# Halves or whole groups: the streams of the first layer of a two-layer decoder

## The reference

```python
x = x + L0_attn(layernorm(x))      # A
x = x + L0_xattn(layernorm(x), ctx, ctx)   # B
x = x + L0_ffn(x)                  # C, D, experts

# A: q = tanh(x Wc + bc), one number a token; shell = l2norm(x Ws + bs), 64 numbers
#    proj = shell omega + bias;  phi_s = [cos(proj), sin(proj)]
#    phi  = (mags * q**[0..4]) outer phi_s, times W_combine -> 64 numbers
#    logits = phi phi^T * decay / temp, causal; softmax; times V; times W_out
# B: one head: q Wq, k = ctx Wk, v = ctx Wv, softmax over 361, times v
# C: h = layernorm(y) with scale and shift; causal attention of 16 heads of 16; wo
# D: h = layernorm(...); scores = h gate_w (8 experts); the two best and a softmax over them
#    experts: silu(h w1) * (h w2), then w3, of 512 hidden, weighted by the gate
```

## Time and profile before

| | us |
|---|---|
| median of the runs | 1693.62 |
| lowest to highest of 3 runs | 1688.9 to 1701.72 |
| profiled execution | 1689.45 |
| its span | 1687.8 |
| front of group 0 alone | 71.2 |
| three woven stretches | 122.9, 123.6, 125.6 |
| rear of group 3 alone | 77.1 |

### The profile page before, as it was taken

One profiled execution on the slowest core, in us unless ns is written; L12 is line 12 of the kernel. 1 busy time (PEld: TensorE's weight loads), 2 busy tenths in 40 slices (PEclk: granted clock), 3 DMA queues, 4 the chain that ended last, 5 costly groups with the idle time before them and its releaser, 6 DMA issues.

```text
span 1687.8 us, 24678 instructions
## 1 busy us (share of the span) xinstructions
PE 1285.4 (76%) x7936; PEld 890.2 (53%) x7936; DVE 998.3 (59%) x2156; ACT 522.3 (31%) x1279; POOL 415.1 (25%) x528
## 2 busy tenths in 40 slices
PE   2677868767877699981458977779787697986987
PEld 1554654644644366651237754467554475644755
DVE  4447557457455233325676765768656686677852
ACT  2214324324322222210125512346213363233620
POOL 1032143243253200006622111311212212032100
PEclk9778878878888799995679989779897799987988
DMA  9510010191014211101315310044100350104501
GB/s 376 217 28 1 19 28 13 34 408 49 25 46 198 59 47 44 44 29 45 117 39 98 86 40 12 10 101 111 40 12 2 86 122 21 32 11 88 114 5 46
DMA packets 69693, 122.37 MB, mean 73 GB/s; under 512 B 25404, under 2 KB 55100, under 8 KB 68032
## 3 DMA queue, kind: packets, MB, share of 16 engines
q1 hardware_dynamic: 63936, 110.04, 21.7%
q0 software_dynamic: 5632, 10.77, 2.3%
HBM read 67.69 MB, written 53.07 MB: 72 GB/s over the span
## 4 chain that ended last, share of the span: by engine, by line
PE 46%; issue 24%; DVE 12%; POOL 8%; DVEq 3%; ACT 3%; DMA 2%; POOLq 2%; SPq 0%; ACTq 0%
PE ps L1143 7%; PE ps L1390 5%; PE ps L1162 3%; PE ps L525 3%; PE ps L1316 3%; PE ps L1332 3%; PE ps L533 2%; POOL experts L1779 2%; PE ps L1302 2%; PE ps L1403 2%; PE ps L933 1%; PE ps L1041 1%; POOL headbd L681 1%; PE ps L504 1%; DVE probs L1999 1%
## 5 line engine op out<-in xcount | busy, mean ns | idle before, releaser
L1628 ACT ACTIVATE probs<-ps,small 100x361 f32<-100x361 f32 x256 | 141.3, 557 | 94.1 <-DVE small L2347 89.5
L2347 DVE TENSOR_REDUCE small<-ps 100x2 f32<-100x722 f32 x128 | 115.7, 906 | 36.2 <-PE ps L1302 36.2
L1143 PE MATMUL ps<-every,xT_t 128*128 x256 | 122.3, 601 | 0.4 <-issue 0.4
L1390 PE MATMUL ps<-hT,experts 128*128 128x400 f32 x288 | 117.1, 558 | 1.2 <-DVE small L730 1.2
L1316 PE MATMUL ps<-cst,probs 100*121 100x100 f32 x768 | 104.0, 271 | 8.1 <-DVE probsT L2355 7.7
L1316 PEld LDWEIGHTS ps<-cst,probs 100*121 100x121 f32 x768 | 94.8, 185 | 22.2 <-issue 13.7
L2355 DVE TENSOR_SCALAR probsT<-ps 121x600 f32<-121x600 f32 x128 | 99.2, 775 | 9.1 <-PE ps L1316 9.1
L1332 PE MATMUL ps<-probsT,values_ 121*32 121x100 f32 x1536 | 90.8, 253 | 0.9 <-DVE probsT L2355 0.9
L1302 PE MATMUL ps<-k_stack,q_stack 96*100 96x362 f32 x256 | 81.8, 400 | 6.3 <-ACT probs L1628 5.6
L473 POOL TENSOR_TENSOR small<-small,cst 100x2 f32<-100x2 f32 x56 | 11.1, 198 | 295.3 <-DVE small L453 295.2
L1390 PEld LDWEIGHTS ps<-hT,experts 128*128 128x128 f32 x288 | 59.6, 215 | 42.2 <-issue 14.1
(11 more groups left out here) (329 smaller groups left out, 2887.2 us busy)
## 6 DMA issues: line engine op xcount, KB each, us to landing
k_stack<-key_d SPq DMA_DIRECT2D x192, 90.5 KB, 3.1
tok_d<-wt SPq DMA_DIRECT2D x1, 14848.0 KB, 45.5
res_d<-wt SPq DMA_DIRECT2D x1, 14848.0 KB, 42.0
every<-e_d SPq DMA_DIRECT2D x8, 1536.0 KB, 11.6
ctxT<-ctxT_d SPq DMA_DIRECT2D x8, 726.0 KB, 4.3
key_d<-k_hi SPq DMA_DIRECT2D x32, 181.0 KB, 2.8
key_d<-k_lo SPq DMA_DIRECT2D x32, 181.0 KB, 3.4
gates<-gate_d SPq DMA_DIRECT2D x28, 200.0 KB, 4.4
```

The lines of the kernel that those rows point to most:

```text
L1143: ins = e.matmul(ps[:, 2 * i + t % 2, :], xT_t[:, t % 2, c, :], every[:, bass.ds(base + (i * DC + c) * HID0, HID0)], start=(c == 0), stop= ...
L1390: ins = e.matmul(bank(2 * i + j % 2, n=NT), w[:, c, :], hT[:, c, :], start=(c == 0), stop=(c == DC - 1))
L1628: ins = e.activation(f_e[:, n % 2, i, 0:LC], bank(2 * (n % 2) + i, S, LC), ACT.Exp, bias=h_nm[:, n % 2, i:i + 1], accum_out=h_sum[:, b, h: ...
L2347: inc(e.tensor_reduce(h_nm[:, n % 2, 0:2], ps[0:S, 2 * (n % 2):2 * (n % 2) + 2, 0:LC], AX, ALU.max, negate=True), "F_nm")
```

## The change

Both parts of the first layer become one stream for a whole group each. `early(g)` has the steps of `early(g, h)`, each for four sequences: one DVE instruction over 400 or 4 x n columns where there were two, one ACT evacuation of a whole group, one POOL power of 100 x 4 for two of 100 x 2. Instructions that stand once for each sequence (statistics, `xn`, exponentials, matrix products of 100 rows) stay as many. `behind(g)` likewise has one step where it had one for each half, and 28 steps instead of 36. `woven(front, rear)` issues, in each of 18 rounds, one front step and then as many rear steps as `REAR_STEPS` says: two in rounds 0 to 3, one in 4 to 6, two in 7 to 12, one in 13 to 17. The attention's 19 steps now lie at rear steps 4 to 22, rounds 2 to 12.

PSUM: the front has banks 0 to 3 as one set, the rear 4 to 7. `A_in` and `A_comb` of all four sequences lie in banks 0 to 3 at once. Names of the first layer are declared with `wholes` and signalled once for a group. The transposed probabilities of B leave in two ACT copies of two sequences each instead of four. `recips_pool` of half 0 moves on POOL from behind the attention into its step 12. SP's three waits are for the whole group's signals; its loads are the same. The front of group 0 is issued as one stream with nothing beside it (`list(early(0))`).

The helpers are `norm4_dve`, `root4_pool`, `turn4_pe`, `turn4_act`, `projT4_pe`, `proj4_pe`. The core of the diff follows: the driver, the helpers, PE's first front steps and its rear up to the attention, two details on ACT and POOL, DVE's `phi`, and DVE's rear.

```diff
-ROUNDS, STEPS = 18, 19
+REAR_STEPS = (2, 2, 2, 2, 1, 1, 1, 2, 2, 2, 2, 2, 2, 1, 1, 1, 1, 1)
+STEPS = 19
...
-def woven(x0, x1, y):
-
-    for _ in range(ROUNDS):
-        for st in (x0, y, x1, y):
-            next(st)
+def woven(front, rear):
+
+    for steps in REAR_STEPS:
+        next(front)
+        for _ in range(steps):
+            next(rear)
...
+        def wholes(name, phase1, phase3="", sem_name=None):
+
+            sem = ctx.enter_context(nc.semaphore(sem_name or name))
+            for i, p in enumerate(phase1):
+                names[f"{p}_{name}"] = Signal(sem, len(phase1), i)
+            for i, p in enumerate(phase3):
+                names[f"{p}_{name}"] = Signal(sem, 2 * len(phase3), len(phase1) * NG + 2 * i, 2)
...
+        def norm4_dve(e, pre, g, src, xn_out):
+
+            stats, mv, _, r1, _, _ = for_y if pre in ("C_", "D_") else for_x
+            for b in range(NB):
+                e.bn_stats(stats[:, b, :], src[:, b, :])
+            e.drain()
+            for b in range(NB):
+                ins = e.bn_aggr(mv[:, b, :], stats[:, b, :])
+            inc(ins, pre + "mv")
+            e.drain()
+            yield
+            W(e, pre + "rstd", g)
+            for b in range(NB):
+                ins = e.tensor_scalar(xn_out[:, b, :], src[:, b, :], mv[:, b, 0:1], r1[:, b:b + 1],
+                                      ALU.subtract, ALU.mult)
+            return ins
+
+        def root4_pool(e, pre, g, eps2=None):
+
+            _, mv, var_e, r1, r2, t1 = for_y if pre in ("C_", "D_") else for_x
+            W(e, pre + "mv", g)
+            e.tensor_tensor(var_e, mv[:, :, 1], cs("eps", S)[:, 0:NB], ALU.add)
+            e.drain()
+            ins = e.tensor_tensor(r1, var_e, cs("mhalf", S)[:, 0:NB], ALU.pow)
+            if eps2 is not None:
+                e.drain()
+                e.tensor_tensor(t1, r1, r1, ALU.mult)
+                e.drain()
+                e.tensor_tensor(t1, t1, mv[:, :, 1], ALU.mult)
+                e.drain()
+                e.tensor_scalar(t1, t1, eps2, None, ALU.add)
+                e.drain()
+                ins = e.tensor_tensor(r2, t1, cs("mhalf", S)[:, 0:NB], ALU.pow)
+            inc(ins, pre + "rstd")
+
+        def part4(b0):
+
+            return ps[:, b0:b0 + 2, 0:NT]
...
+        def turn4_pe(e, pre, g, name, b0, src, ready, half=0):
+
+            W(e, ready, g, 1, half)
+            for c in range(DC):
+                for b in range(NB):
+                    ins = e.transpose(ps[:, b0 + c, b * S:(b + 1) * S], src[:, b, c * P:(c + 1) * P], identS)
+            inc(ins, pre + name)
...
+        def projT4_pe(e, w, src, b0, name):
+
+            for m in range(DC):
+                for c in range(DC):
+                    ins = e.matmul(bank(b0 + m, n=NT), w[:, c, m * P:(m + 1) * P], src[:, c, :],
+                                   start=(c == 0), stop=(c == DC - 1))
+            inc(ins, name)
+
+        def proj4_pe(e, w, srcT, b0, name):
+
+            for b in range(NB):
+                for c in range(DC):
+                    ins = e.matmul(ps[0:S, b0 + b // 2, b % 2 * D:(b % 2 + 1) * D], srcT[:, c, b * S:(b + 1) * S],
+                                   w[:, c, :], start=(c == 0), stop=(c == DC - 1))
+            inc(ins, name)
...
 
-            def early(g, h):
-                p, q, t, bs = 2 * h, 2 * h + 1, tok(h), list(enumerate(seqs(h)))
-                yield
-                turn_pe(e, "A_", g, h, "hTp", p, xnX, ("A_xn", 1))
-                yield
-                W(e, "A_hT", g, 1, h)
+            def early(g):
+                yield
+                turn4_pe(e, "A_", g, "hTp", 0, xnX, "A_xn")
+                yield
+                W(e, "A_hT", g)
                 w = wv("A_in", DC)
-                for i, b in bs:
+                for b in range(NB):
                     for c in range(DC):
-                        ins = e.matmul(bank(p + i, S, 321), hTX[:, c, b * S:(b + 1) * S], w[:, c, :],
+                        ins = e.matmul(bank(b, S, 321), hTX[:, c, b * S:(b + 1) * S], w[:, c, :],
                                        start=(c == 0), stop=(c == DC - 1))
                 inc(ins, "A_in_p")
...
+                    ins = e.matmul(bank(b, S, 320), a_trig[:, b * S:(b + 1) * S], wv("A_comb", rows_=SH),
                                    start=True, stop=True)
                 inc(ins, "A_comb")
...
                         scores(n)
@@ -1081,42 +1137,38 @@
                 yield
                 if routed:
                     ahead(g - 1)
-                yield
-                for h in range(2):
-                    turn_pe(e, "C_", g, h, "hTp", 4 + 2 * h, xn, ("C_xn", 1))
-                    yield
-                for h in range(2):
-                    W(e, "C_hT", g, 1, h)
-                    if h == 1 and routed:
-                        e.wait_ge(r_placed.sem, r_placed.at(g - 1))
-                    proj_pe(e, h, wv("C_v", DC), hT, 5 + 2 * h, "C_vp")
-                    projT_pe(e, h, wv("C_k", DC), hT, 4 + 2 * h, "C_kTp")
-                    yield
-                for h in range(2):
-                    W(e, "C_v", g, 1, h)
-                    projT_pe(e, h, wv("C_q", DC), hT, 5 + 2 * h, "C_qTp")
+                turn4_pe(e, "C_", g, "hTp", 4, xn, "C_xn")
+                yield
+                W(e, "C_hT", g)
+                if routed:
+                    e.wait_ge(r_placed.sem, r_placed.at(g - 1))
+                proj4_pe(e, wv("C_v", DC), hT, 6, "C_vp")
+                projT4_pe(e, wv("C_k", DC), hT, 4, "C_kTp")
+                yield
+                W(e, "C_v", g)
+                projT4_pe(e, wv("C_q", DC), hT, 6, "C_qTp")
                 yield
                 yield from attend(g)
-                for h in range(2):
-                    turn_pe(e, "C_", g, h, "rTp", 4 + 2 * h, xn, ("C_rx", 1))
-                    yield
-                for h in range(2):
...
-                W(e, "B_pTp", g, 1, h)
-                for i, b in enumerate(seqs(h)):
-                    ins = e.activation(b_eT[:, b, :], bank(p + i, KW, KC * S), ACT.Copy)
+                W(e, "B_pTp", g)
+                for b in range(0, NB, 2):
+                    ins = e.activation(b_eT[:, b:b + 2, :], ps[0:KW, b:b + 2, 0:KC * S], ACT.Copy)
...
+                    if n == 12:
+                        recips_pool(e, "C_", g, 0, 1)
...
-                W(e, "A_comb", g, 1, h)
-                W(e, "A_q", g, 1, h)
-                phi = a_phi[:, o, :]
-                qb = a_q[:, o].unsqueeze(2).broadcast_to([S, HB, SH])
-                pm = lambda m: ps[0:S, p:p + 2, m * SH:(m + 1) * SH]
-                e.tensor_scalar(phi, pm(ORD - 1), MAGS[ORD - 1] / MAGS[ORD - 2], None, ALU.mult)
+                W(e, "A_comb", g)
+                W(e, "A_q", g)
+                qb = a_q.unsqueeze(2).broadcast_to([S, NB, SH])
+                pm = lambda m: ps[0:S, 0:NB, m * SH:(m + 1) * SH]
+                e.tensor_scalar(a_phi, pm(ORD - 1), MAGS[ORD - 1] / MAGS[ORD - 2], None, ALU.mult)
                 e.drain()
                 for m in range(ORD - 2, -1, -1):
                     if m == ORD - 2:
-                        e.tensor_tensor(phi, phi, qb, ALU.mult)
+                        e.tensor_tensor(a_phi, a_phi, qb, ALU.mult)
                     else:
-                        e.scalar_tensor_tensor(phi, phi, MAGS[m + 1] / MAGS[m], qb, ALU.mult, ALU.mult)
+                        e.scalar_tensor_tensor(a_phi, a_phi, MAGS[m + 1] / MAGS[m], qb, ALU.mult, ALU.mult)
                     e.drain()
-                    ins = e.tensor_tensor(phi, phi, pm(m), ALU.add)
+                    ins = e.tensor_tensor(a_phi, a_phi, pm(m), ALU.add)
                     if m:
                         e.drain()
                 inc(ins, "A_phi")
                 yield
...
                 ways = route(g - 1) if routed else iter(())
                 group = xall[:, bass.ds(g * NB, NB), :]
-                norms = [norm_dve(e, "C_", g, h, group, y) for h in range(2)]
-                next(norms[0])
+                norm = norm4_dve(e, "C_", g, group, y)
+                next(norm)
                 next(ways, None)
                 yield
-                next(norms[1])
-                yield
-                for h in range(2):
-                    list(norms[h])
-                    e.drain()
-                    for b in seqs(h):
-                        ins = e.tensor_scalar(xn[:, b, :], y[:, b, :], r2Y[:, b:b + 1], None, ALU.mult)
-                    inc(ins, "C_xn")
-                    if h == 0:
-                        next(ways, None)
-                    yield
-                for h in range(2):
-                    W(e, "C_vp", g, 1, h)
-                    inc(e.tensor_scalar(c_v[:, own(h), :], tokens(5 + 2 * h), 1.0, None, ALU.mult), "C_v")
-                    yield
+                list(norm)
+                e.drain()
+                for b in range(NB):
```

(40 more changed lines are left out.)

423 lines of the change are left out of this document (197 added, 226 removed).

## The result

The changed kernel took 1736.69 us (median of 4 runs, 1736.21 to 1741.99), the kernel before 1691.69 us in the runs beside it. The ratio is 1.0262 with a 95% interval of 1.0214 to 1.0310: 45 us slower. The profiled execution has a span of 1735.1 us against 1687.8, so 47.3 us more.

The account below looks back on a forecast made before the run. PE was taken as nearest to a bound, 93 of 124 us busy in a woven stretch. Woven +12.3, front +20, rear +3.6 made +35.9 us: 1689.45 to 1725.4 profiled, 1729 as median, range 1686 to 1754.

Parts of the forecast that it names:

- the wait for `A_shn`: Rounds 2 to 6 of a woven stretch: PE waits over 3 us for this input from DVE; a 4 us gap.
- the front alone: Front of group 0 with nothing woven in, 71.2 us before: engines' times add to 91, +20 us.
- the woven stretches: Three stretches weaving one group's rear with the next front: +4.1 us each, 12.3 together, 126 to 130 long.
- the waits for Sin and `phi`: Rounds 4 and 5 of a woven stretch: PE waits 2 and 2.4 us by the sum, over 3 each as sign.
- (a): Woven stretch, first statistics to first attention scores, 32.4 us before: -0.7 us.
- (b): Woven stretch, first attention scores to stage A's logits in round 7, 25.1 us before: +3.9 us.
- (c): Woven stretch, stage A's logits to last attention values, rounds 7 to 12, 39.8 us before: +2.2 us.
- (d): Woven stretch, last attention values to the next group's statistics, 26.3 us before: -1.3 us.
- rear alone: Rear of group 3 with nothing woven in, 77.1 us before: end is a bare chain, +3.6 us.
- B: Rival for the whole kernel: DVE's chain is the bound everywhere, so not slower; 1677 us, chance 0.17.
- C: Rival: weaving is even, gaps in (b) and (c) paid by (a) and (d), only ends lose; 1706 us, chance 0.20.
- D: Rival: PE's clock falls and stays, +10 us a woven stretch, ends +28; 1752 us, chance 0.15.

Follow-up runs that it names:

- steps_late: Changed kernel, rear steps reordered: one in rounds 0 to 2, two in 3 to 12, one in 13 to 17; 1717.01 us, ratio 1.0140 to the kernel before.
- steps_early: Changed kernel, rear steps reordered: two in rounds 0 to 9, one in 10 to 17; 1751.08 us, ratio 1.0358 to the kernel before.
- tail_warm: Changed kernel with filler matrix products on PE in the last rear only; 1738.21 us, ratio 1.0271 to the kernel before.
- rear_halves: Changed kernel with the rear back in half streams, 36 steps, two a round, front whole; 1710.71 us, ratio 1.0086 to the kernel before.
- warm_all: Changed kernel with filler matrix products on PE in group 0's front alone and in the woven rounds; 1733.64 us, ratio 1.0232 to the kernel before.

## Why the prediction held, point by point

The direction, the size and the range were right: 1729 predicted, 1736.7 measured, slower by more than 1%. Part of that is luck. The sum is a worse forecast than its total: it put the first layer at +36 where +60 were measured, and the total came near because code that it took as unchanged was 12.6 us shorter. Of the signs named ahead, the wait for `A_shn`, round 10 and DVE's busy time came; the front alone (85 to 95 us), the woven stretches (126 to 130) and the waits for Sin and `phi` (over 3 us) did not. What the sum had too small is in each of these places mostly one term, PE's work at the lower clock. By its own terms, against profiled stretches:

| term | predicted | measured |
|---|---|---|
| front alone | +20 (8 to 24) | +25.9 |
| (a) of a woven stretch | -0.7 | -0.8 |
| (b) | +3.9 | +4.8 |
| (c) | +2.2 | +6.9 |
| (d) | -1.3 | -0.9 |
| three woven stretches | +12.3 | +25.8 |
| rear alone | +3.6 | +7.9 |
| first layer | +35.9 | +60 |
| code behind it | 0 | -12.6 |

- **Front alone.** The mechanism was right: in one stream the engines' times add. The sum of 93 less 2 of overlap came to 97.1. PE's work grew to 53.0 at a clock of 0.68, 5.1 more than the 47.9 of the earlier trace rows that the sum had kept. ACT was busy 15.8 and not 12.4: the sum took off three table loads, but both kernels have three in this stretch. More overlap than 2 us hid a part of that. The upper bound of 95 for half clock throughout does not follow from its own lower bound: if full clock takes 12 us off PE's 47.9, half clock makes them about 72, and the bound about 115.
- **(a), (b) and (d)** were each within 1 us. In (a) the terms add up to 32.4, no change; the -0.7 was set lower for the stretch in which nothing is routed, so that the routed one gave -0.8 is chance. In (b) the wait for `A_shn` is there with 4.6 us, as forecast; those for Sin and `phi` are 2.1 and 2.0, near the 2 and 2.4 of the sum and not over 3. PE's front steps of rounds 3 to 6 began 6.4, 12.8, 17.7 and 26.1 us after the first scores, where 6.4, 13.0, 17.8 and 24.5 were predicted; the last is late behind a round at a clock of 0.60. The reason given for (b), one rear step as too little cover, is not borne out as it stands: (a) and (b) of `steps_late`, with two rear steps in rounds 4 to 6, are together 4.0 us shorter, but `steps_early`, also with two, is 12.0 longer in (b).
- **(c) is the step that failed.** Its rounds 7, 9 and 10 were counted well (7.2, 6.2 and 11.7 us; 7.9, 6.5 and 12.0 predicted), but with 0.4 us for the clock in the whole part. Round 10, from `A_out` to the next transposes:

```profile
331.98 3.71 PE L535 MATMUL ps<-wt,experts 128*100 128x256 f32 x16
...
343.70 1.60 PE L509 MATMUL ps<-cst,experts 100*128 100x100 f32 x8 [1.28 <-DVE experts L478]
```

  PE was busy 37.8 us there at 0.78, against 31.7 at 0.96 in the earlier trace rows: 6.1 of the 6.9 us. Round 8 took 6.9 us for 5.0 predicted, at 0.55, and rounds 11 and 12 took 14.7 for 10.2, at 0.59; the same instructions in the same order took 5.5 and 11.6 in `steps_late`. The clock term of (c) was thus about 4.4 and not 0.4. The sum took (c)'s clock over from before, though it placed new gaps on PE in the same rounds and had seen in the earlier trace rows that a gap can bring the lower level.
- **Rear alone.** The tail of whole steps grew by 7.3 us (23.2 from the last values to the routing, 15.9 before), where 3.1 was predicted; the 21.6 in the expectation of `tail_warm` is too small. `C_out` was costed at 3.5, full clock, and took 6.6; the gate's scores, costed at 1.6 in (d), took 2.8. These two make up the 4.2 us that the sum lacked. `tail_warm` did not test whether full clock would give them back, as its filler stood in the way.
- **POOL.** `root4_pool`'s power of 100x4 took 1.05 us, between the bounds of 0.75 and 1.5 and near the 1.2 taken:

```profile
L488 POOL TENSOR_TENSOR small<-small,cst 100x4 f32<-100x4 f32 x4 | 4.2, 1050 | 1.6 <-issue 1.5
```

- **DVE** saved 30.3 us of busy time in the first layer, 24 predicted, while every stretch grew.
- **The code behind** was taken as unchanged. It was 12.6 us shorter, and that hid half of the error in the first layer. Nothing in the prediction leads there.
- **The rivals.** B, DVE's chain as the bound, is excluded: DVE's busy time fell and every stretch grew. C, woven stretches even, is what `steps_late` (376.1) and `rear_halves` (377.0) come to, not the changed kernel. D, the clock falls and stays, put the stretches at +10 each, the first layer at +58 and the total at 1752. In the profile the woven stretches rose by 8.6 each with the clock at 0.77, and the first layer by 60: by place and size D is closer to the first layer than the forecast, and only the shorter code behind it put the total on the forecast's side. D's cause is shown for (c), by 4.4 of its 6.9 us. It is not shown for all: with the clock back at 0.83 in `warm_all` two thirds of the loss stayed, about half of that from its filler by the estimate above, and `steps_late` has 0.78 in a stretch only 2.8 us longer than before. The rule of the Trainium skill cited with D ("TensorE: Matmul & The Clock Gate", section "HAM oscillation — how this bites in real kernels"), that idle gaps send the array back to half rate, agrees with these rows as far as the lower clock goes.

## What to carry to other kernels

Two interleaved half streams are each other's cover: made into one, every engine's step stands in the open wherever nothing else is woven in, and that price (26 and 8 us at the two ends here) did not depend on the order of the woven steps, while the saved fixed cost per instruction (30 us on DVE) shortened no stretch, as DVE was not the bound. In a hand-written order the list of steps is as large a lever as the steps: the same instructions took 376 to 434 us, so a change of grain has to be timed with its order tried anew, not with the first list that fits. Cost every matmul behind a gap at both clocks. Filler is a test of the clock only where it fits its gap: it was worth 9 us in one stretch, and in another it delayed the chain by as much as it gave. Two kernels that issue the same instructions in the same order from some point on are the cleaner test.

## What was not expected of the hardware

- Code with the same instructions took 1111.5 to 1125.2 us over the kernels of this study, with granted clocks of 0.87 and 0.95 on the same 40 us of attention, and with stalls of 6 us on DVE that no semaphore explains. Runs of one kernel scatter as much (1687.2 to 1705.2 us for the kernel before), while the three woven stretches of the changed kernel's code took 397.8 or 397.9 us in three builds. A difference under 14 us between two profiled executions is not evidence about the edit until the stretch that was edited is cut out.
- Mean clock and length part ways: from 0.77 to 0.83 by filler gave 3.3 us of 133.6 in a woven stretch, and from 0.80 to 0.84 none in the last rear, while another order of the steps gave 7.2 us at 0.78.
- An order of steps reaches beyond itself: rounds 8, 11 and 12, the same in every instruction, took 4.4 us less in `steps_late`, at clocks of 0.69 and 0.79 instead of 0.55 and 0.59.
- A power of 100x4 on POOL takes 1.05 us where 100x2 takes 0.75. By these two, an estimate: 0.45 us fixed and 0.15 for each column.
